# Perceiver block on one core: x normalised ahead of the weights' low part, the second step's query and keys in banks of their own, ScalarE's reorder of the roots and two sums of roots on VectorE

## The reference, cut to what matters

```python
# x (2, 256, 256), ctx_1024 (2, 4096, 256), all float32
x = x + _L0_xattn_ref(_layernorm(x), ctx_1024, ctx_1024, w_q, w_k, w_v, w_o)  # 16 heads of 64, softmax(q k / 8) v
x = x + _L0_attn_ref(_layernorm(x), wq, wk, wv, wo)      # 16 heads of 16, softmax(-dist)
x = x + _L0_ffn_ref(_layernorm(x), Wg, bg, W1, b1, W2, b2)

# in _L0_attn_ref:
cosh_arg = 1.0 + 2.0 * c * diff_sq / denom
return jnp.arccosh(jnp.maximum(cosh_arg, 1.0))           # exp(-arccosh) are the weights
```

## Time and profile before

| | us |
|---|---|
| median of 3 runs | 1114.92 (1113.4 to 1120.04) |
| the profiled execution | 1119.39 |
| its span, first to last instruction | 1117.7 |
| PE busy | 1042.0 (93%) |
| DVE busy | 813.9 (73%) |
| ACT busy | 793.5 (71%) |
| POOL busy | 676.8 (61%) |
| PE's share of the chain that ended last | 81% |

### The profile page before, as it was taken

How to read it: one execution, slowest core, us unless ns; L and a number is a source line. 1 busy time by engine, 2 the same in 40 slices (tenths; PEclk the granted TensorE clock), 3 DMA queues, 4 the chain that set the end, 5 groups by cost and what they waited for, 6 DMA issues and landing times.

```text
span 1117.7 us, 36600 instructions
## 1 busy us (share of the span) xinstructions
PE 1042.0 (93%) x15401; PEld 779.4 (70%) x15401; DVE 813.9 (73%) x1059; ACT 793.5 (71%) x1452; POOL 676.8 (61%) x613
## 2 busy tenths in 40 slices
PE   5799999999999999999999999999999999767688
PEld 3376777777777777777777777777777777543476
DVE  3887887777778777777777777777767759557442
ACT  5486777777777777777777777777776756798754
POOL 5365666666666666666666666676665556834233
PEclk9999999999999999999999999999999999797699
DMA  5921320000000000000000000003000010000000
GB/s 202 254 41 35 64 54 7 16 7 17 7 17 7 16 7 16 7 17 7 16 7 16 8 16 7 17 7 120 7 3 7 16 63 3 2 1 1 1 1 20
DMA packets 50932, 31.73 MB, mean 28 GB/s; under 512 B 27194, under 2 KB 47698, under 8 KB 50770
## 3 DMA queue, kind: packets, MB, share of 16 engines
q1 hardware_dynamic: 50770, 29.39, 9.9%
HBM read 22.57 MB, written 0.52 MB: 21 GB/s over the span
## 4 chain that ended last, share of the span: by engine, by line
PE 81%; DVE 8%; issue 4%; ACT 3%; POOL 2%; DMA 1%; SPq 0%; ACTq 0%; POOLq 0%; DVEq 0%
PE ps L1443 15%; PE ps L1388 14%; PE ps L1525 13%; PE ps L1472 6%; PE ps L1571 5%; PE ps L1566 5%; PE ps L1569 5%; PE ps L1513 4%; PE ps L809 2%; PE ps L769 2%; POOL psums L2126 2%; PE ps L1504 1%; PE ps L1373 1%; PE ps L585 1%; DVE m_part L1933 1%
## 5 line engine op out<-in xcount | busy, mean ns | idle before, releaser
L2126 POOL TENSOR_TENSOR psums<-probs 128x512 f16<-128x512 f32 x512 | 590.7, 1174 | 330.7 <-ACT probs L1767 277.0
L1758 ACT ACTIVATE probs<-ps 128x512 f32<-128x512 f32 x512 | 279.7, 600 | 193.2 <-PE ps L1525 192.3
L1933 DVE TENSOR_REDUCE m_part<-ps 128x2 f32<-128x1024 f32 x256 | 312.7, 1224 | 136.2 <-PE ps L1472 134.9
L1767 ACT ACTIVATE probs<-probs 128x512 f16<-128x512 f32 x384 | 242.0, 632 | 0.3
L1525 PE MATMUL ps<-q_hi,k_p 64*128 64x256 f16 x2048 | 211.2, 269 | 0.0
L1566 PE MATMUL ps<-v_sb,probs 128*128 128x65 f16 x2048 | 205.3, 192 | 4.5 <-POOL psums L2126 4.5
L1569 PE MATMUL ps<-v_sb,probs 128*128 128x64 f16 x2048 | 205.3, 192 | 0.0
L1571 PE MATMUL ps<-v_sb,psums 128*128 128x65 f16 x2048 | 204.8, 194 | 0.0
L1566 PEld LDWEIGHTS ps<-v_sb,probs 128*128 128x128 f16 x2048 | 188.4, 98 | 19.6 <-POOL psums L2126 6.1
L1569 PEld LDWEIGHTS ps<-v_sb,probs 128*128 128x128 f16 x2048 | 188.0, 97 | 16.0
L1571 PEld LDWEIGHTS ps<-v_sb,psums 128*128 128x128 f16 x2048 | 188.2, 97 | 0.0
(11 more groups left out here) (248 smaller groups left out, 1680.4 us busy)
## 6 DMA issues: line engine op xcount, KB each, us to landing
ctx_hi<-in_L_ffn_W_dram SPq DMA_DIRECT2D x2, 2048.0 KB, 9.9
probs<-in_ctx_dram SPq DMA_DIRECT2D x4, 512.0 KB, 7.6
wqk_raw<-in_L_xattn_w_q_dram SPq DMA_DIRECT2D x16, 128.0 KB, 2.3
wqk_raw<-in_L_xattn_w_k_dram SPq DMA_DIRECT2D x16, 128.0 KB, 2.8
k_p<-in_ctx_dram SPq DMA_DIRECT2D x4, 512.0 KB, 11.4
wv_raw<-in_L_xattn_w_v_dram SPq DMA_DIRECT2D x16, 128.0 KB, 2.7
wo_raw<-in_L_xattn_w_o_dram SPq DMA_DIRECT2D x16, 128.0 KB, 2.0
ctx_hi<-in_ctx_dram SPq DMA_DIRECT2D x7, 256.0 KB, 5.6
```

The costliest lines, as they stand in the source:

```text
L1758: nc.scalar.activation(p_raw[:, s:s + 2, h, :], ps[:, score_bank(n, pair, h), :].rearrange("p (k q) -> p k q", k=2), ACT.Exp, scale=XSCALE ...
L1767: nc.scalar.activation(p_hi[:, s % NP, :, :], p_raw[:, s % NX, :, :], ACT.Copy) \
L1933: nc.vector.tensor_reduce(m_part[:, j, t, :], ps[:, bank:bank + 2, :], AX.X, ALU.max) \
L2126: nc.gpsimd.tensor_tensor(p_lo[:, s % NP, :, :].rearrange("p h q -> p (h q)"), p_raw[:, s % NX, :, :].rearrange("p h q -> p (h q)"), p_hi[ ...
```

## The change

Four things. On DVE `normalised(0)` moves ahead of `split_k(0)`. In the last turn of the first loop `subtract_high(7)` moves behind `maxima(14)`, and `project_q(1)` comes there too, ahead of `maxima(15)`, into bank 2 (SECOND_Q); `project_k(0, 1)` writes bank 3 (SECOND_K); the two waits of PE on `s_kl` are gone; DVE takes the maxima and the keys' low half ahead of the query's. In the tail ACT's list is reordered (`weights(2)` ahead of `take_average(0)`, the averages spread among the first roots, `roots(6)` ahead of `take_turned`, `weights(4)` ahead of `gates(0)`), and three of PE's and DVE's places move one distance later. The sums of roots of groups 6 and 7 go from POOL to DVE, with a semaphore `s_rb` of their own.

```diff
+SECOND_Q, SECOND_K = 2, 3
-AVERAGE_AFTER = {4: (0, None), 6: (1, 0), 8: (2, 1), 9: (3, 2), 10: (None, 3)}
-TURN_AFTER, PROJECT_AFTER, NORMALISE_AFTER = 13, 15, 11
+AVERAGE_AFTER = {4: (0, None), 6: (1, 0), 8: (2, 1), 9: (3, 2), 11: (None, 3)}
+TURN_AFTER, PROJECT_AFTER, NORMALISE_AFTER = 14, 15, 12
+        def q_bank(n):
+            return (MX, SECOND_Q)[n] if n < 2 else PV
...
-            for gg in range(8):
+            for gg in range(6):
                 pool.wait_ge(s_r2, gg + 1)
                 nc.gpsimd.tensor_tensor(ratio[gg], root_of(gg), ratio[gg], ALU.add) \
                     .then_inc(s_ra, 1)
...
             def logarithms(gg):
-                act.wait_ge(s_ra, gg + 1)
+                if gg < 6:
+                    act.wait_ge(s_ra, gg + 1)
+                else:
+                    act.wait_ge(s_rb, gg - 5)
...
             weights(1)
+            weights(2)
             take_average(0)
-            weights(2)
+            weights(3)
             take_average(1)
-            weights(3)
+            root_of_product(4)
             take_average(2)
-            roots(4)
+            root_of_sum(4)
             take_average(3)
             roots(5)
+            roots(6)
             take_turned(1, 0, OUT_BANKS[0][0])
-            for gg in range(6, 8):
-                roots(gg)
+            roots(7)
...
+            weights(4)
             gates(0)
-            for gg in range(4, 8):
+            for gg in range(5, 8):
                 weights(gg)
...
+            def sum_of_roots(gg):
+                dve.wait_ge(s_r2, gg + 1)
+                nc.vector.tensor_tensor(ratio[gg], root_of(gg), ratio[gg], ALU.add).then_inc(s_rb, 1)
+
+            sum_of_roots(6)
             residual(0)
             variance(3, slice(0, 2))
             normalised(3, slice(0, 2))
+            sum_of_roots(7)
...
-                if j >= BY_PE:
+                if BY_PE <= j < KCH - 1:
                     subtract_high(j)
...
                 maxima(2 * j, 0, 0)
+                if j == KCH - 1:
+                    subtract_high(j)
+                    project_q(1, 1, ORDER[1][1])
                 maxima(2 * j + 1, 0, 0)
-            pe.wait_ge(s_kl, KCH - 1)
-            project_q(1, 1, ORDER[1][1])
-            pe.wait_ge(s_kl, KCH)
-            project_k(0, 1, 1, ORDER[1][1], PK)
+            project_k(0, 1, 1, ORDER[1][1], SECOND_K)
...
             variance(0, slice(0, NT))
+            normalised(0, slice(0, NT))
             split_k(0, 0)
-            normalised(0, slice(0, NT))
...
+            take_max(0)
+            take_k(0, 1, 1, SECOND_K)
             take_q(1)
-            take_max(0)
-            take_k(0, 1, 1, PK)
```

More of the change, by code:

```diff
@@ L340, in perceiver @@
         s_ge = sem("s_ge")
+        s_rb = sem("s_rb")
         s_bt = sem("s_bt")
@@ L1372, in project_q @@
                 for c in range(NC):
-                    mm = pe.matmul(ps[:, PV if n else MX, 0:TQ], wqk_raw[:, par, 0, c, :],
+                    mm = pe.matmul(ps[:, q_bank(n), 0:TQ], wqk_raw[:, par, 0, c, :],
                                    xnT[:, c, b * TQ:(b + 1) * TQ],
@@ L1711, in take_q @@
                 act.wait_ge(s_q, n + 1)
-                nc.scalar.activation(q_hi[:, n % 3, :], ps[:, PV if n else MX, 0:TQ], ACT.Copy) \
+                nc.scalar.activation(q_hi[:, n % 3, :], ps[:, q_bank(n), 0:TQ], ACT.Copy) \
                     .then_inc(s_qh, 1)
@@ L1916, in take_q @@
                 dve.wait_ge(s_qh, n + 1)
-                nc.vector.tensor_tensor(q_lo[:, n % 3, :], ps[:, PV if n else MX, 0:TQ], q_hi[:, n % 3, :],
+                nc.vector.tensor_tensor(q_lo[:, n % 3, :], ps[:, q_bank(n), 0:TQ], q_hi[:, n % 3, :],
                                         ALU.subtract).then_inc(s_ql, 1)
```

## The result

| | before | after |
|---|---|---|
| median, us | 1117.83 (11 runs, 1113.4 to 1120.27) | 1108.83 (11 runs, 1107.74 to 1111.91) |
| ratio of after to before | | 0.9928 [0.9914, 0.9941] |
| the profiled execution | 1119.39 | 1110.04 |
| its span | 1117.7 | 1108.3 |

The account below looks back on a forecast made before the run. PE was at work 93% of the span, so only opening and tail could give: 5.0 + 2.3 + 4.1 = 11.4 us off the median of 1114.92 gives 1103.5, own range 1101.0 to 1106.7, widened to 1099.5 to 1109.

Parts of the forecast that it names:

- The opening: First term, up to x normalised and what follows: 4.5 us earlier, taken as 5.0 with a possible clock gain, bounds 4.2 to 5.8.
- 2.67 of order: Opening: with the weights' low half behind `xn`, the reciprocal starts at 6.86 for 9.53, 2.67 us earlier.
- 1.8 of stall: Opening: `xn` ended at 13.7 instead of 11.9 because DVE stood still until POOL's instruction was done.
- The end of the loop: Second term, last reductions to step 0: gain of 2.6 with PE's clock high or 1.4 with it low; 2.3 taken.
- The tail: Third term, first distance to last exponential: exponentials end 2.4 + 1.7 = 4.1 us earlier, bounds 2.6 to 5.5.
- hangs on ACT as before: Behind the tail's exponentials: best expert's mask, biases and last average were said to depend on ACT unchanged.
- the tail's lower bound, 2.6: Tail: gain of only 2.6 us if the stretch behind it runs at the low clock where it had the high one.
- within one per cent (0.54): Whole kernel: chance 0.54 of a change within one per cent, 11.15 us, what a measurement can tell from no change.
- The transfers: Rival, opening: the transposing transfers catch the gain, part one brings about 1.5, time 1107; chance 0.12.
- The sums: Rival, tail: sums on DVE delay residual and logits, the tail brings about 1.5, time 1106; chance 0.14.
- The second part: Rival, end of the loop: the second part does nothing, time 1105.8; chance 0.06.
- Slower: Rival, steps: PE is granted 1.2 GHz more often, 14 further stretches, time 1127 or above; chance 0.03.

Follow-up runs that it names:

- part one alone: Kernel before with only `normalised(0)` moved ahead of `split_k(0)` on DVE: 1114.5 us for 1117.96, ratio 0.9971.
- Alone, the part: Kernel before with only the second step's query and keys in banks 2 and 3, query between two tiles of maxima: 1114.26 us, ratio 0.9973.
- alone, in the old order: Kernel before with only the sums of roots of groups 6 and 7 moved to DVE: 1116.37 us for 1116.69, ratio 1.0.
- either half alone: Kernel before with only the tail's two sums on DVE: 1116.37 us, ratio 1.0; or only the tail's reordering, sums on POOL: 1119.41, ratio 1.0018.

## Why the prediction missed

**The opening, 5.0 predicted (4.2 to 5.8): this is the step that failed, by its size and not by its mechanism.** In the two profiles all is as worked out: `xn` at 9.23 (9.25 predicted), four pieces of 0.35, first reduction at 19.76 (19.6), 4.85 us earlier. But the 2.67 of order and the 1.8 of stall were read from one execution in which the weights landed late, at 8.72, and where they land by 7.52 there is no stall and the order is worth 1.2. Over eight executions of the old opening and five of the new the difference is 11.74 - 9.35 = 2.4 us (part one alone measured 3.2, 1.8 to 4.8 by its interval). The prediction had a clue: it noted that the profiled execution lay 4.5 above the median of three runs, and still took its whole 11.4 off that median. What the change removed was a good part of why the opening of that execution was slow. The clue was weaker than it seemed, since the median of eleven runs is 2.9 higher and the profiled execution only 1.6 above it. Taken off the profiled execution, 11.4 gives 1108.0; that of the changed kernel took 1110.04. That the median came out near 1108.0 too, at 1108.83, is in part luck: the experts' loss and the gain of step 0, both left out of the sum, work against each other.

**The end of the loop, 2.3 predicted.** From the reductions to step 0 it went from 8.82 to 6.55, 2.3 us, with query and keys at the high clock, as the prediction leaned to. Over all executions it is 8.46 (nine) to 6.56 (five), 1.9, because two of the nine had no stretch at 1.2 GHz there. A gain not in the sum came with it: a second 1.2 GHz stretch, near 104 us, costs step 0 1.1 us; seven of nine executions with the old order have it and two of five with the new. Alone, the part measured 3.0.

**The tail, 4.1 predicted.** 51.2 went to 46.7 in the one profile and to 47.1 in the four others with the new tail, 4.5 and 4.1; in the means over all executions 4.4 (two of the seven with the old tail took 51.6 and 51.7). The steps hold: the ratios end 2.7 earlier, the projection takes its 3.78 at the low clock, the sum took 2.28 (2.3 to 2.4 predicted), and the idle piece before the gate, 1.69, is gone.

**What the sum left out** is behind the tail. It says that what follows "hangs on ACT as before", and allows for the low clock there only in the tail's lower bound, 2.6. It does hang on ACT, but PE's dense stretches are granted a different clock. The experts took 51.4 in six of seven executions with the old tail (54.6 in one) and 53.0, 53.1 and 54.8 with the new one. In the means, 51.9 and 53.6, that is 1.7 us back.

By the profiles' means 2.4 + 1.9 + 0.4 (step 0) + 4.4 - 1.7 = 7.4 us; by the ratios 8.0 and 9.4. The executions are few, and where the remaining 1 to 2 us come from is not settled.

**The rivals.** The transfers did not catch the gain: the last one takes 4.55 from 29.33 for 4.49 from 34.18. The sums were not in the way, though alone, in the old order, one is, by 0.3 us. The second part was not worth nothing. Slower it was not; the extra stretches at 1.2 GHz are real, but they fell among the experts, two rather than fourteen, and not in the steps. The chances leaned the right way, to within one per cent (0.54), but gave 0.43 to more than that, which rested on the oversized first term.

## What to carry to other kernels

A change is worth its mean over executions, and a profile is one of them: before a wait is priced from one trace, ask whether it hangs on something that varies, such as the landing of a transfer, and take several traces of the kernel before if it does. Where the profile lies well above the median and the change removes what made it slow, the gain read from it can't be taken off the median whole. A short instruction that stands behind a transfer and just ahead of a long one of another engine that stalls it has two outcomes; putting it clear of both narrows the spread as well as lowering the time. Test the halves of a reorder apart: here either half alone brought nothing or less at the end of the kernel, and only together did they pay.

## What was not expected of the hardware

The landing time of the same 128 KB transfer, issued at the same 2.33 us, varied from 4.84 to 6.89 us over the fourteen executions profiled. With the old order DVE turned 4.91 to 6.75 into `xn` ready anywhere from 10.44 to 14.08; with the new one 4.84 to 6.89 became 9.21 to 9.53.

A variance of two columns took 4.28 us for 0.17 where it met POOL's sum of 2048 columns, the largest such stall in these traces.

The 1.2 GHz stretches are not fixed to a place in the program: at the end of the first loop seven of nine executions of the old order had one and two had none, with the same instructions, and among the experts the unedited kernel took 51.4 three times and 54.6 once. The kernel spreads over some 8 us in 29 runs. The start of the last four reductions (up to 4.2 us apart in the four executions of before), the end of the loop with step 0 (up to 2.9) and the experts (3.2) are large enough for that together, but how they combine in single runs is not shown; of 58 runs of before, the seven with the highest granted clock, 0.976 or above, took 1113.6 to 1117.1, the lower half of the spread.
